# Expert stages of a two-layer token kernel: thirteen tiles of 640 tokens become ten of 832

## What is computed

```python
# layer 0: H = 256, relu, softmax over the two best of Wg x + bg
# layer 1: H = 170, silu(w1 x) * (w3 x), sum of the two best router weights normalised
n = norm(x)
y = sum(weight[e] * (W2[e] @ act(W1[e] @ n)) for e in two_best(router(n)))
x = x + y
```

## Time and profile before

| | us |
|---|---|
| median of 3 runs | 1122.05 (1120.3 to 1124.96) |
| span of the profiled execution | 1120.4 |
| expert stages of layer 0, first to last up matmul | 224.3 to 524 |
| expert stages of layer 1, first to last up matmul | about 766.5 to 1105.7 |
| busy: TensorE / VectorE / ScalarE / GpSimd | 1041.2 / 856.0 / 610.7 / 446.2 |

### The profile page before, as it was taken

The page is one execution under the profiler, slowest core; times in us unless marked ns, Lnnn a source line. Parts: engine busy times, 40 slices in busy tenths (PEclk is TensorE's granted clock), DMA queues, the critical chain, the costliest instruction groups (busy, mean ns, idle before and its releaser), DMA issues. The chain is left out here.

```text
span 1120.4 us, 24166 instructions
## 1 busy us (share of the span) xinstructions
PE 1041.2 (93%) x8747; PEld 764.9 (68%) x8747; DVE 856.0 (76%) x2048; ACT 610.7 (55%) x1321; POOL 446.2 (40%) x595
## 2 busy tenths in 40 slices
PE   6897889699999999999888799988999999999996
PEld 2475756477777777776665477755777777777774
DVE  2786959867777777778877589956788888888876
ACT  2375645565665555566337567755554554455452
POOL 3224402304443444434357577800244333344433
PEclk9898999989999999999989999999999999999999
DMA  8200000000000000000001000000000000000000
GB/s 230 126 1 2 2 1 2 1 1 1 1 1 1 1 1 2 1 1 1 1 24 42 8 2 2 3 2 1 1 7 7 13 8 7 7 8 7 7 7 12
DMA packets 5236, 15.56 MB, mean 14 GB/s; under 512 B 608, under 2 KB 3936, under 8 KB 4736
## 3 DMA queue, kind: packets, MB, share of 16 engines
q1 hardware_dynamic: 4784, 9.97, 3.1%
q0 software_dynamic: 336, 4.07, 0.9%
HBM read 11.91 MB, written 2.13 MB: 13 GB/s over the span
## 5 line engine op out<-in xcount | busy, mean ns | idle before, releaser
L1522 PE MATMUL moe_psU<-moe_nT_parts,moe_w_hi 128*128 128x320 f32 x988 | 324.5, 339 | 4.5 <-DVE moe_hid L1425 2.3
L1522 PE MATMUL moe_psU<-moe_nT_parts,moe_w_lo 128*128 128x320 f32 x988 | 296.5, 310 | 0.0
L1522 PEld LDWEIGHTS moe_psU<-moe_nT_parts,moe_w_hi 128*128 128x128 f32 x988 | 187.5, 190 | 60.6 <-issue 50.3
L1522 PEld LDWEIGHTS moe_psU<-moe_nT_parts,moe_w_lo 128*128 128x128 f32 x988 | 188.4, 191 | 0.0
L1419 DVE TENSOR_TENSOR moe_hid<-moe_psU,moe_silu 128x320 f32<-128x320 f32 x286 | 139.1, 491 | 49.8 <-ACT moe_silu L1193 40.7
L1093 POOL TENSOR_TENSOR moe_sum<-moe_scaled 128x256 f32<-128x256 f32 x124 | 93.5, 754 | 161.7 <-DVE moe_scaled L1409 161.4
L1193 ACT ACTIVATE moe_silu<-moe_psU 128x320 f32<-128x320 f32 x286 | 125.4, 439 | 56.1 <-PE moe_psU L1522 39.2
L1198 ACT ACTIVATE moe_hid<-moe_psU,middle 128x320 f32<-128x320 f32 x260 | 129.4, 527 | 30.9 <-PE moe_psU L1522 28.9
L1425 DVE TENSOR_SCALAR moe_hid<-moe_psU,middle 128x320 f32<-128x320 f32 x156 | 85.5, 549 | 55.8 <-PE moe_psU L1522 54.9
L1533 PE MATMUL moe_psY<-moe_hid,late 128*64 128x320 f32 x832 | 123.4, 439 | 0.9 <-DVE moe_hid L1419 0.9
L1533 PE MATMUL moe_psY<-moe_hid,middle 128*64 128x320 f32 x832 | 123.4, 439 | 0.7 <-ACT moe_hid L1198 0.7
(11 more groups left out here) (356 smaller groups left out, 1932.2 us busy)
## 6 DMA issues: line engine op xcount, KB each, us to landing
images<-in_x SPq DMA_DIRECT2D x8, 576.0 KB, 11.1
late<-in_late POOLq DMA_DIRECT2D x1, 2263.5 KB, 11.3
out_tokens<-h SPq DMA_DIRECT2D x13, 160.0 KB, 1.8
middle<-in_middle POOLq DMA_DIRECT2D x1, 1554.0 KB, 6.9
project_turns<-in_turns SPq DMA_DIRECT2D x8, 160.0 KB, 2.2
early<-in_early SPq DMA_DIRECT2D x1, 1043.0 KB, 19.0
turns_first<-in_turns SPq DMA_DIRECT2D x4, 160.0 KB, 2.5
turns_first<-in_turns POOLq DMA_DIRECT2D x1, 160.0 KB, 11.5
```

The source lines that it names most:

```text
L1522: last = pe.matmul(psum[:, 0:HALF], w[:, col:col + SPLIT], moving, start=(part == 0), stop=(part == 1))
```

## The change

Tiles of the expert stages become 6.5 slots, 832 tokens (`MTOK`), with halves of 416 columns (`MHALF`), and there are NMT = 10 of them. A pair of tiles covers 13 slots: of norm and router an even tile takes 7 slots and an odd one 6 (`taken_slots`), and the outputs of an even tile are given back as 6 slots and those of an odd one as 7 (`given_slots`). The units, their number in a tile and their order stay as they are. The buffers grow with the tile; y becomes one buffer of two tiles side by side.

The places at which slots are turned back and weighed are new. In layer 0 the turned outputs come two slots at a time at (0,7), (1,4) and (2,1), and a seventh at (2,6). In layer 1 they come one at a time, in two different lists for tiles that give 7 and 6. `SLOTS`, `DOWN`, `LOGITS`, `HI`, `KEEP` and `EXP` keep their values, and the order inside a place is the same. In the tail POOL_LAST is 3, and slots beyond the free banks go to `psM` again. What runs ahead of a stage (the norm of its first tile) works on 7 slots.

```diff
+MT = 7
+PAIR_SLOTS = 2 * MT - 1
+MTOK = PAIR_SLOTS * B // 2
+MHALF = MTOK // 2
+NMT = 2 * L // PAIR_SLOTS
+def taken_slots(g):
+    return PAIR_SLOTS * (g // 2) + g % 2 * MT, MT - g % 2
+def given_slots(g):
+    return PAIR_SLOTS * (g // 2) + g % 2 * (MT - 1), MT - 1 + g % 2
...
-        y = [sb(f"y{k}", [128, PAIRS, TOK]) for k in range(2)]
+        y = sb("y", [128, PAIRS, 2 * MTOK])
-        psU = [ps(f"psU{k}", 128, HALF) for k in range(4 if layer == 0 else 5)]
+        psU = [ps(f"psU{k}", 128, MHALF) for k in range(4 if layer == 0 else 5)]
...
-        POOL_LAST = 2
+        POOL_LAST = 3
+        FREE = 3 if layer == 0 else 5
...
         if layer == 0:
             LOGITS, DOWN = (0, 2), 4
-            OUTS = [(0, 7), (1, 2), (1, 7), (2, 2), (2, 6)]
+            OUTS = [(0, 7), (0, 7), (1, 4), (1, 4), (2, 1), (2, 1), (2, 6)]
-            WEIGH = [(0, 7), (1, 3), (1, 7), (2, 3), (2, 7)]
+            WEIGH = [(0, 7), (1, 0), (1, 4), (1, 6), (2, 1), (2, 3), (2, 7)]
+            OUTS, WEIGH = {MT: OUTS, MT - 1: OUTS[:-1]}, {MT: WEIGH, MT - 1: WEIGH[:-1]}
             SLOTS = {(0, 4): "aannnnnn", (1, 4): "naaaaaa", (2, 4): "naaaaaaa", (3, 4): "eeeeee"}
         else:
             LOGITS, DOWN = (0, 0), 1
-            OUTS = [(0, 3), (1, 0), (1, 3), (2, 0), (2, 2)]
+            OUTS = {MT: [(0, 3), (0, 5), (1, 1), (1, 3), (1, 5), (2, 0), (2, 2)], MT - 1: [(0, 3), (1, 0), (1, 2), (1, 5), (2, 0), (2, 2)]}
             WEIGH = OUTS
...
             SLOTS = {(0, 1): "aaaannn", (1, 1): "neeeeee", (2, 1): "neeeeee", (3, 1): "eeeeeee"}
...
                         if before:
-                            for t in range(T):
-                                if OUTS[t] == (p, k):
+                            for t, place in enumerate(OUTS[given_slots(g - 1)[1]]):
+                                if place == (p, k):
...
                     if not ending:
-                        need(pe, scaled_set, g * T + max(t + 1 - MBANKS, 0))
+                        need(pe, scaled_set, given_before(g) + max(t + 1 - MBANKS, 0))
```

More of the change, by code:

```diff
@@ L938, with over_bodies, given_before @@
 TOP_TWO_LINKS = 11
-def over_bodies(eng, body, chain=None, per=0):
-    def counted(start, steps, call):
+def over_bodies(body, chain=None, per=0):
+    for g in range(NMT - 1):
         if chain is not None:
[L945 to L952, removed]
+            chain.enter(0, per)
+        body(g, g > 0, True)
         if chain is not None:
             chain.leave(1)
+PAIR_SLOTS = 2 * MT - 1
+MTOK = PAIR_SLOTS * B // 2
+MHALF = MTOK // 2
+NMT = 2 * L // PAIR_SLOTS
+assert NMT * PAIR_SLOTS == 2 * L
+def taken_slots(g):
+    return PAIR_SLOTS * (g // 2) + g % 2 * MT, MT - g % 2
+def given_slots(g):
+    return PAIR_SLOTS * (g // 2) + g % 2 * (MT - 1), MT - 1 + g % 2
+def given_before(g):
+    return given_slots(g)[0] if g < NMT else L
 def moe(nc, layer, late, early, src, resid, out, minus_half, first, ahead=None):
@@ L1016, in moe @@
-        sum4, sum2, sum1 = sb("sum4", [B, T, 4 * D]), sb("sum2", [B, T, 2 * D]), sb("sum1", [B, T, D])
+        nTr = [sb(f"nT_parts{k}", [128, 2 * MTOK], F32R) for k in range(2)]
+        nrm, split = sb("nrm", [B, MT, D]), sb("split", [B, MT, 128])
+        cen, sq, stats = sb("cen", [B, MT, D]), sb("sq", [B, MT, D]), sb("stats", [B, 3, MT])
+        hid = [sb(f"hid{k}", [128, MHALF]) for k in range(NHID)]
+        sil = [sb(f"silu{k}", [128, MHALF]) for k in range(3)] if layer else None
+        y = sb("y", [128, PAIRS, 2 * MTOK])
@@ L1017, in moe @@
+        scaled = sb("scaled", [B, MT, E * D])
+        sum4, sum2, sum1 = sb("sum4", [B, MT, 4 * D]), sb("sum2", [B, MT, 2 * D]), sb("sum1", [B, MT, D])
         weights = sb("weights", [B, L, E])
-        small = {k: sb("r_" + k, [B, T, E]) for k in "val eq ranked left first second d prob".split()}
-        tiny = {k: sb("r_" + k, [B, T]) for k in "m0 m1 m2 best diff ex den rec w2 sum".split()}
-        psU = [ps(f"psU{k}", 128, HALF) for k in range(4 if layer == 0 else 5)]
+        small = {k: sb("r_" + k, [B, MT, E]) for k in "val eq ranked left first second d prob".split()}
@@ L1021, in moe @@
+        tiny = {k: sb("r_" + k, [B, MT]) for k in "m0 m1 m2 best diff ex den rec w2 sum".split()}
+        psU = [ps(f"psU{k}", 128, MHALF) for k in range(4 if layer == 0 else 5)]
         psY_both = ps("psY", 128, 1024)
-        psY = psY_both[:, :].rearrange("p (x n) -> p x n", x=2)[:, :, 0:HALF]
+        psY = psY_both[:, :].rearrange("p (x n) -> p x n", x=2)[:, :, 0:MHALF]
         MBANKS = 2 - layer
         psM = ps("psM", 128, MBANKS * 512)
-        LOGITS_AT = TOK if layer == 0 else 128
@@ L1117, in _ @@
                 deviation(1)
-                for g in range(1, NT - 1):
-                    chain.enter(0, 3 * T + layer)
+                for g in range(1, NMT - 1):
+                    chain.enter(0, 3 * given_slots(g - 1)[1] + layer)
                     deviation(g + 1)
@@ L1140, in _ @@
                 if layer == 1:
-                    with sp.Fori(0, NT) as g:
+                    for g in range(NMT):
+                        s0, n = given_slots(g)
                         sp.wait_ge(added, g + 1)
-                        sp.dma_start(out[:, bass.ds(g * T, T), :], resid[:, bass.ds(g * T, T), :]).then_inc(stored, 16)
-                    sp.wait_ge(stored, 16 * NT)
+                        sp.dma_start(out[:, s0:s0 + n, :], resid[:, s0:s0 + n, :]).then_inc(stored, 16)
+                    sp.wait_ge(stored, 16 * NMT)
             @block.scalar
@@ L1237, in tables_ahead, with body @@
                     act.wait_ge(through_set, 3)
-                def body(g, slot, before, front):
+                def body(g, before, front):
                     for p, k, u in places():
@@ L1486, in transposes @@
                     if part == 0:
-                        need(pe, scaled_set, (g - 1) * T)
+                        need(pe, scaled_set, given_before(g - 1) if g else 0)
                     else:
-                        pe.wait_ge(nTr_set, g * len(TURNS) + part)
+                        pe.wait_ge(nTr_set, g * PARTS + part)
                     for t in range(t0, t1):
@@ L1492, in transposes, with logits, up @@
                     last.then_inc(T_mm, 1)
-                def logits(g, slot):
-                    pe.wait_ge(nTr_set, (g + 1) * len(TURNS))
-                    need(pe, scaled_set, (g - 1) * T)
-                    for t in range(T):
-                        at = LOGITS_AT + t * 2 * E
-                        last = pe.matmul(psM[:, at:at + 2 * E], nTr[slot][:, t * B:(t + 1) * B], w_gate[:, :], start=True, stop=True)
+                def logits(g):
+                    pe.wait_ge(nTr_set, (g + 1) * PARTS)
+                    need(pe, scaled_set, given_before(g - 1) if g else 0)
+                    for t in range(taken_slots(g)[1]):
+                        at, begin = LOGITS_AT + t * 2 * E, turned_columns(g) + t * B
+                        last = pe.matmul(psM[:, at:at + 2 * E], nTr[g // 2 % 2][:, begin:begin + B], w_gate[:, :], start=True, stop=True)
                     last.then_inc(L_mm, 1)
-                def up(g, slot, u, first_tile=False):
+                def up(g, u, first_tile=False):
                     p, half, chunk = units[u]
-                    moving = nTr[slot][:, half * HALF:(half + 1) * HALF]
+                    begin = g % 2 * MTOK + half * MHALF
+                    moving = nTr[g // 2 % 2][:, begin:begin + MHALF]
                     if u == 0 or layer == 1 and half == 1 and units[u - 1][1] == 0:
-                        pe.wait_ge(nTr_set, g * len(TURNS) + (half + 1 if layer == 1 else 1))
+                        pe.wait_ge(nTr_set, g * PARTS + (half + 1 if layer == 1 else 1))
                     if first_tile and u == first_of[p]:
@@ L1521, in up @@
                         for part, w in enumerate((w_hi, w_lo)):
-                            last = pe.matmul(psum[:, 0:HALF], w[:, col:col + SPLIT], moving, start=(part == 0), stop=(part == 1))
+                            last = pe.matmul(psum[:, 0:MHALF], w[:, col:col + SPLIT], moving, start=(part == 0), stop=(part == 1))
                         last.then_inc(done, 1)
@@ L1567, in through_weights_ahead, with body @@
                     last.then_inc(through_mm, 1)
-                def body(g, slot, before, front):
+                def body(g, before, front):
                     for p, k, u in places():
-                        up(g, slot, u, not before)
+                        up(g, u, not before)
                         if (p, k) == LOGITS:
@@ L1592, in body @@
                             transposes(g + 1, 1)
-                for part in range(len(TURNS)):
+                for part in range(PARTS):
                     if part:
@@ L1597, in _ @@
                     transposes(0, part)
-                over_bodies(pe, body)
-                body(NT - 1, 0, True, False)
-                down(NT - 1, PAIRS - 1)
+                over_bodies(body)
+                body(NMT - 1, True, False)
```

(9 more changed lines are left out.)

240 lines of the change are left out of this document (128 added, 112 removed).

## The result

The changed kernel takes 1136.33 us (median of 4 runs, 1136.07 to 1139.5), the kernel before 1123.33 beside it: ratio 1.014, 95% interval 1.0102 to 1.0178. It is slower by 1.4% (the two medians alone differ by 1.2%). The profiled execution spans 1134.2 us, 13.8 more than before. The forecast was 1138, within 1124 to 1149.

The account below looks back on a forecast made before the run. TensorE was taken to set the tile's period, VectorE keeping up under its long down projections. Tiles -15.7, ends +4.7 and waits +27.4 gave +16.4 on a 1120.4 us span, 1136.8; median forecast 1138, range 1124 to 1149.

Parts of the forecast that it names:

- tile of layer 0 without waits: Layer 0's tile period from TensorE's work alone: 29.06 us, against 22.95 before with smaller tiles.
- tile of layer 1 without waits: Layer 1's tile period from TensorE's work alone: 33.26 us, against 26.19 before with smaller tiles.
- waits in layer 0: At (2,1), TensorE waits 1.8 us to turn slot 5 until slot 3 is weighed, in nine tiles: 16.2 us.
- waits in layer 1: TensorE waits 2.3 us in four tiles giving 7 slots (9.2) and 0.4 in five giving 6 (2.0).
- ends: Longer tails, heads and last store, less slots that leave the tile bodies: +4.7 us, bounds nothing to 8.
- Fewer, wider matmuls: Both expert stages: 456 fewer up matmuls and 24 fewer downs save TensorE per-matmul and stage-change time, -15.7 us together.
- Two slots at a time saves TensorE nothing: Layer 0's paired turning back: a turned slot costs nothing for the change of stage, so pairing gains nothing.
- Small steps lose their cover: At a down's place VectorE weighs first, so its seven steps no longer run beside the down; waits in all +27.4 us.
- X: Start of turning slot 2 at a down's place; in layer 0 slot 5 can start at X + 4.98, TensorE arrives X + 3.18.
- VectorE would be done in time: Rival: VectorE finishes its steps before TensorE reaches (2,1) and (1,5), so no waits: 1111 us, chance 0.17.
- one layer alone would wait: Rival: only one layer's waits come, 1127 us for layer 0 alone or 1122 for layer 1 alone; chance 0.11.
- Up matmuls that scale with columns: Part of the heavier rival: nothing saved on up matmuls, +6.2 us; with stretched steps (+5) 1149 us, chance 0.14.

Follow-up runs that it names:

- e1: Changed kernel with VectorE's small norm and router steps put before the weighing where a down projection is issued, both layers: 1116.47 us, ratio 0.9975.
- e6: e1 with two units or a down between any two slots turned back in layer 1: 1113.21 us, ratio 0.9936 to the kernel before.
- e5: e1 with layer 0's slots turned back one at a time at seven places instead of in pairs: 1116.24 us, ratio 0.9974.
- e2: Changed kernel with the small steps before the weighing at a down's place in layer 0 alone: 1124.43 us, ratio 1.0024.
- e3: Changed kernel with the small steps before the weighing at a down's place in layer 1 alone: 1130.17 us, ratio 1.0103.
- e4: Kernel before, 13 tiles, with layer 0's slot 1 turned back and weighed at (1,4), a down's place: 1143.99 us, ratio 1.0224.

## Why the prediction was right

By its steps, forecast against measured:

| step | forecast | measured | from |
|---|---|---|---|
| tile of layer 0 without waits | 29.06 | 29.06 | e1, windows |
| tile of layer 1 without waits | 33.26 | 33.40 | e6, windows |
| all tiles without waits, against before | -15.7 | 290.6 + 334.0 - 298.4 - 340.5 = -14.3 | the two rows above |
| waits in layer 0 | 16.2 | 9 x 1.59 = 14.3 | after less e1, windows |
| waits in layer 1 | 11.2 | 341.6 - 330.2 = 11.4 | after less e6, first to last up matmul |
| ends | +4.7 | 13.8 + 14.3 - 14.3 - 11.4 = +2.4 | what is left of the span |
| span | +16.4 | +13.8 | profiled executions |

The mechanism is shown, and the number is near because every term is: the largest misses are 2.3 in the ends and 1.9 in layer 0's waits, both too high, against 1.4 too much credit for the tiles.

*Fewer, wider matmuls.* Right in mechanism, and nearly in size: the up distance keeps most of its fixed part at 416 columns, a down costs 3.14 for 3.15, and tiles without waits come out within 0.14 us. That the distance is 0.188 and not 0.187 is 1.5 us in 1520 up matmuls, as much as the miss of 1.4 here. The end of the range at which nothing is saved on the up matmuls is excluded by 0.188 against 0.191. The Trainium skill's fixed 2.5 ns (TensorE: Matmul & The Clock Gate, Wait — 56ns, not 53.3ns?) agrees with the traces in that a part of the distance barely grows with the columns, and not in its size: 13.7 and 14.7 ns are measured in these float32r streams.

*Two slots at a time saves TensorE nothing.* Shown by e5, within 0.05 us a tile.

*Small steps lose their cover.* Shown three times: by undoing the order (e1), by layer (e2, e3), and by making the same loss in the kernel before (e4). The forecast's reading was a little too neat: the steps stood beside the down for 1.4 of their 2.2 us, not for all of them. Each wait in layer 0 was put at 1.8 and is 1.6: slot 5 came 4.79 after X, not 4.98, and TensorE was there at 3.27, not 3.18. The steps were counted too long: they hold VectorE 2.19 (297.30 to 299.49) where 2.17 + 0.13 + 0.1 = 2.40 was taken, since norm and router never both work on 7 slots at this place. The forecast's own terms add up to X + 4.93, not 4.98. In layer 1 the three places of the wait are the forecast's, (1,5), slot 4 and slot 5, with 1.0, 0.6 and 0.35 for 1.1, 0.74 and 0.45. Of the 11.4 us of layer 1's waits the order gives 7.0 back (e1) and the spacing 4.5 (e6), from the first up matmul to the last.

*Ends.* Taken as +4.7. In layer 1's tail the slope is as worked out (+0.87 in the reduction, +0.14 in the addition, two more weighings), but by remainder the ends are +2.4. The traces say where the rest is. Outside the two expert stages the kernel after is 7.4 us longer: 0.6 ahead of layer 0's first up matmul, 4.0 between the stages and 2.8 behind layer 1's last. (The stretch between the stages differs by 2.0 between the kernel before and e4 too, where its code is the same, so the 4.0 is uncertain by that much.) Inside, from first to last up matmul, the tiles without waits of e1's layer 0 and e6's layer 1 take 19.3 us less than before, 5.0 more than the 14.3 of whole periods. A period holds work that the first or the last tile lacks: the 2 x 2 slots that the forecast counted, 1.7, and the last down of each stage, which stands behind the last up matmul, 2 x 0.64 = 1.3. The other 2.0 are not taken apart, and they are about what the term missed.

*The rivals.* That VectorE would be done in time was wrong for the kernel as it stands. e6 shows its time: a profiled span of 1109.0, 11.4 under the kernel before, where this rival has 11.0; the medians measured beside each other differ by less, 1113.21 and 1119.77. That one layer alone would wait is refuted by e2 and e3. Up matmuls that scale with columns are excluded by the distance above. That the norm's step stretches beside GpSimd's sums is real, as the last section shows, but at the place that decides in layer 0 it took its short time, 0.55 for 384 columns, and in layer 1 no more than 0.85, where it had 0.89 before.

## What to carry to other kernels

In this kernel the small work of VectorE was free only while nothing that TensorE soon needed stood behind it in the same queue. So before an instruction that must wait for a long one of the bounding engine is put into a second engine's queue, list what stands behind it there, and which of that the bounding engine will ask for. That VectorE was idle for a quarter of layer 0's time before (193.24 busy of 252.50 us) didn't help, since its queue runs in order: the same instructions in another order moved the time by some 20 us. When a tile size and an order written by hand change together, test them apart: the size gained 14 us in the tiles, and the waits at the new places took 26 back.

## What the runs showed that I had not expected

The norm's multiplication in layer 1 took 0.89 us for 320 columns before, against 0.48 in layer 0. In the changed kernel it takes 0.55 for 384 and 0.85 for 448, and in e1, where only the order differs, 0.67 for 384. GpSimd's timeline, beside VectorE's, says what it meets. Kernel before, then e1:

```profile
879.61 0.73 POOL L1093 TENSOR_TENSOR moe_sum<-moe_scaled 128x256 f32<-128x256 f32 x1 [0.49 <-DVE moe_scaled L1409]
879.81 0.89 DVE L1305 TENSOR_TENSOR moe_nrm<-n_all,moe_stats 128x320 f32<-128x320 f32 x1
```

```profile
836.64 0.46 POOL L1128 TENSOR_TENSOR moe_sum<-moe_sum 128x128 f32<-128x128 f32 x1 [0.18 <-POOL moe_sum L1126]
836.84 0.67 DVE L1344 TENSOR_TENSOR moe_nrm<-n_all,moe_stats 128x384 f32<-128x384 f32 x1
```

Where a sum of GpSimd is already running when the step starts, the step is longer by what the sum has left, less some 0.13. In the first pair the sum has 0.53 left and the step takes 0.40 more than 0.48; in the second it has 0.26 left and the step takes 0.12 more than 0.55. Where no sum is running at its start the step has its short time: 0.48, 0.55 and 0.61 for 320, 384 and 448 columns, in the traces of before, after and e1. It holds the other way round too: a sum that starts 0.23 into the step takes 0.92 instead of 0.73 (kernel after, layer 0, at 297.53). No experiment moved this alone, so it is a reading of the traces; it cost nothing here that TensorE had to wait for, beyond what the table has.

The medians of one and the same kernel before range from 1119.77 to 1123.33 between groups of runs, more than half of what e6 gains; only a ratio to the kernel before measured beside it carries that gain.
